# Head stacks of an attention layer: how their parts lie in DRAM, how they are loaded, and when each half is waited for

## The reference

```python
q1, q2, k, v = (split_heads(x @ W) for W in (Wq1, Wq2, Wk, Wv))   # 16 heads of 16 features
q = concatenate([q1, q2], heads)          # 32 query heads
k2, v2 = repeat(k, 2), repeat(v, 2)       # query heads 2n and 2n+1 share key head n
p = softmax(causal(q @ k2.T / 4))
y = p @ v2
y = y[:, :16] - sigmoid(x @ Wlam) * y[:, 16:]
x = layernorm(x + y @ Wo)
x = layernorm(x + shared_mlp(x) + routed_mlp(x) * comb_w)   # comb_w from a top-2 router
```

## Time and profile before

| | |
|---|---|
| median of three runs | 504.79 us |
| profiled execution, own time | 504.88 us |
| span of its instructions | 503.1 us |
| TensorE busy | 424.3 us (84%) |
| VectorE busy | 329.1 us (65%) |
| ScalarE busy | 239.1 us (48%) |
| GpSimd busy | 226.7 us (45%) |
| mean granted TensorE clock | 0.950 |
| DMA, hardware queue q1 | 34304 packets, 39.75 MB |

### The profile page before, as it was taken

One profiled execution on the slowest core, in us unless ns is written; L12 is line 12 of the kernel. 1 busy time (PEld: TensorE's weight loads), 2 busy tenths in 40 slices (PEclk: granted clock), 3 DMA queues, 4 the chain that ended last, 5 costly groups with the idle time before them and its releaser, 6 DMA issues.

```text
span 503.1 us, 10443 instructions
## 1 busy us (share of the span) xinstructions
PE 424.3 (84%) x4008; PEld 337.4 (67%) x4008; DVE 329.1 (65%) x875; ACT 239.1 (48%) x532; POOL 226.7 (45%) x283
## 2 busy tenths in 40 slices
PE   4107597799999999999899999999999988997983
PEld 4106335676688758876798668865887578766983
DVE  3504615974478577877687677857786769676674
ACT  4601284337435672548334843576255821582240
POOL 8201466427435572547434743656254721373040
PEclk9756779889999999999999999999999999999998
DMA  8892496129603680249112940377024910000000
GB/s 290 188 123 49 126 137 150 44 75 124 89 4 114 91 121 23 75 92 135 51 42 78 141 90 12 107 97 119 20 79 74 133 46 0 5 2 22 1 23 21
DMA packets 34355, 40.43 MB, mean 80 GB/s; under 512 B 3840, under 2 KB 27904, under 8 KB 34048
## 3 DMA queue, kind: packets, MB, share of 16 engines
q1 hardware_dynamic: 34304, 39.75, 43.2%
HBM read 27.94 MB, written 11.53 MB: 78 GB/s over the span
## 4 chain that ended last, share of the span: by engine, by line
PE 69%; DVE 15%; DMA 5%; ACT 5%; issue 4%; POOL 2%; SPq 1%; DVEq 0%
PE ybank L734 10%; PE ff L622 9%; PE ff L624 8%; PE ff L623 8%; DVE neg_max L990 8%; PE ring L706 5%; PE ring L685 5%; DMA k_stack<-qk_parts_dram 4%; PE ybank L622 4%; PE ybank L747 3%; PE ring L710 3%; PE ybank L623 3%; PE ybank L624 3%; ACT prob L469 2%; PE ring L680 2%
## 5 line engine op out<-in xcount | busy, mean ns | idle before, releaser
L990 DVE TENSOR_REDUCE neg_max<-ring 128x2 f32<-128x512 f32 (+3 forms) x176 | 105.7, 635 | 39.2 <-PE ring L685 37.4
L469 ACT ACTIVATE prob<-ring 128x512 f32<-128x512 f32 x192 | 100.8, 612 | 15.9 <-PE ring L706 15.8
L370 POOL TENSOR_TENSOR h_lo<-h_full,h_hi 128x256 fp32r<-128x256 f32 x72 | 53.0, 736 | 107.7 <-ACT h_hi L429 107.7
L380 POOL TENSOR_SCALAR_AFFINE_SELECT prob<-prob 128x512 f32<-128x512 f32 x128 | 83.9, 679 | 33.9 <-ACT prob L469 33.9
L622 PE MATMUL ff<-x1T_hi,wg_lo 128*128 128x256 f32 x288 | 85.8, 298 | 1.2 <-DVE h_full L1006 1.2
L624 PE MATMUL ff<-x1T_hi,wg_hi 128*128 128x256 f32 x288 | 80.5, 279 | 0.0
L623 PE MATMUL ff<-x1T_lo,wg_hi 128*128 128x256 f32 x288 | 80.5, 279 | 0.0
L680 PE MATMUL ring<-mask_b,ident_b 128*128 128x128 bf16 (+2 forms) x176 | 45.2, 257 | 32.7 <-DMA k_stack<-qk_parts_dram 26.8
L477 ACT ACTIVATE gate_t<-ff 128x256 f32<-128x256 f32 x72 | 27.6, 384 | 77.2 <-PE ff L624 74.5
L685 PE MATMUL ring<-k_stack,q_stack 96*128 96x256 bf16 (+3 forms) x512 | 60.5, 239 | 0.0
L734 PE MATMUL ybank<-prob,v_ones 128*32 128x256 f32 (+1 forms) x1024 | 56.1, 338 | 4.2 <-issue 2.8
(11 more groups left out here) (150 smaller groups left out, 947.9 us busy)
## 6 DMA issues: line engine op xcount, KB each, us to landing
q_stack<-qk_parts_dram SPq DMA_DIRECT2D x48, 256.0 KB, 9.2
qk_parts_dram<-parts SPq DMA_DIRECT2D x72, 128.0 KB
k_stack<-qk_parts_dram SPq DMA_DIRECT2D x8, 384.0 KB, 15.0
xt_raw<-xT SPq DMA_DIRECT2D x8, 256.0 KB, 2.9
k_stack<-qk_parts_dram SPq DMA_DIRECT2D x8, 256.0 KB, 11.8
xz<-x SPq DMA_DIRECT2D x8, 256.0 KB, 3.3
out<-xz SPq DMA_DIRECT2D x8, 256.0 KB, 2.2
prob<-w_gu SPq DMA_DIRECT2D x1, 1152.0 KB, 7.7
```

The source lines that it names most:

```text
L370: pool.tensor_tensor(h_lo[:, n, :], h_full[:, n % RING, :], h_hi[:, n, :].bitcast(F32), ALU.subtract).then_inc(h_lo_done, 1)
L380: pool.affine_select(out=v, in_=v, compare_op=ALU.is_ge, fill=0.0, base=0, pattern=[[0, 2], [HALF, 2], [0, 2], [1, HALF]], channel_multipl ...
L469: act.activation(prob[:, g % RING, u, :], ring[u][:, :], ACT.Exp, scale=SCALE).then_inc(exp_done, 1)
L990: dve.tensor_reduce(neg_max[:, columns.start:columns.stop, i], ring[u % RING][:, 0:len(columns) * keys].rearrange("p (h k) -> p h k", k=keys),
```

## The change

The parts of q and of k get DRAM tensors of their own, `q_parts_dram` with the two q jobs kept apart and `k_parts_dram`. In both, the eight heads of a block with 512 values each follow each other, a run of 8 KB for one feature. `q_stack` is laid out to match: first the block, then the head in it.

The slots that hold the same part are filled by one load: three copies of the high part, two of the middle one, one of the low one (`Q_RUNS`). The source of such a load repeats with a stride of zero in its outermost dimension: source `[0, 3], [8192, 16], [1, 4096]` (stride, count), destination `[8192, 48], [1, 1], [1, 4096]` for the three copies. Each covers one q job, so there are six q loads in a sequence as before, now 3 + 3 by halves, beside the three k loads, whose runs are now 8 KB.

The order of the projections becomes q (first half of the heads), k, q (second half); `Q_JOB` and `K_JOB` name them, and the host puts the weight columns in that order. The loads are in two groups with a semaphore each. `load_first_half` needs only the first two jobs, and `load_second_half` the third one. TensorE waits for the first group ahead of unit 0 and for the second ahead of unit 11. The 22 units are reordered accordingly: eleven for heads 0 to 7 (1, 2, 4 and 4 units by query tile), then the same for heads 8 to 15. The third projection moves from after unit 10 to after unit 11. At the start of the program the order on SP changes too.

```diff
-Q_PARTS = (0, 0, 0, 1, 1, 2)
-K_PARTS = (0, 1, 2, 0, 1, 0)
-SLOTS = len(Q_PARTS)
+Q_JOB, K_JOB = (0, 2), 1
+EARLY_JOBS = K_JOB + 1
+Q_RUNS = ((0, 3), (3, 2), (5, 1))
 K_RUNS = ((5, 1), (3, 2), (0, 3))
-S_JOBS = tuple((i, j) for i, heads in enumerate(S_TILE_HEADS) for j in range(HEADS // heads))
+S_JOBS = tuple((i, q * (BLOCK_HEADS // heads) + j)
+               for q in range(Q_JOBS) for i, heads in enumerate(S_TILE_HEADS) for j in range(BLOCK_HEADS // heads))
-QK_AT = (3, 6, 10)
+QK_AT = (3, 6, 11)
-        scratch = nc.dram_tensor("qk_parts_dram", [3, HEAD_DIM, BLOCK_HEADS, QK_JOBS, 2 * T], BF16, kind="Internal").ap()
+        scratch_q = nc.dram_tensor("q_parts_dram", [3, HEAD_DIM, Q_JOBS, BLOCK_HEADS, 2 * T], BF16, kind="Internal").ap()
+        scratch_k = nc.dram_tensor("k_parts_dram", [3, HEAD_DIM, BLOCK_HEADS, 2 * T], BF16, kind="Internal").ap()
...
-                for p in range(3):
-                    sp.wait_ge(parts_stored[p], (b + 1) * (16 * QK_JOBS))
-                    for s in range(SLOTS):
-                        if Q_PARTS[s] == p:
-                            sp.dma_start(q_stacks[b % STACKS][HEAD_DIM * s:HEAD_DIM * (s + 1), :, :, :], scratch[p, :, :, 0:Q_JOBS, :]).then_inc(stack_loaded, 16)
-                    s, count = K_RUNS[p]
-                    sp.dma_start(k_stacks[b % STACKS][HEAD_DIM * s:HEAD_DIM * (s + count), :, :, :],
-                                 scratch[0:count, :, :, Q_JOBS, :].rearrange("p d r t -> (p d) r t")).then_inc(stack_loaded, 16)
+            def load_q(b, q, p):
+                s, count = Q_RUNS[p]
+                sp.dma_start(q_stacks[b % STACKS][HEAD_DIM * s:HEAD_DIM * (s + count), q, :, :].rearrange("p r t -> p (r t)"),
+                             scratch_q[p, :, q, :, :].rearrange("d r t -> d (r t)").unsqueeze(0).to_broadcast([count, HEAD_DIM, BLOCK_HEADS * 2 * T])).then_inc(stack_loaded[q], 16)
+            def load_k(b, p):
+                s, count = K_RUNS[p]
+                sp.dma_start(k_stacks[b % STACKS][HEAD_DIM * s:HEAD_DIM * (s + count), :, :, :].rearrange("p r h t -> p (r h t)"),
+                             scratch_k[0:count].rearrange("p d r t -> (p d) (r t)")).then_inc(stack_loaded[0], 16)
+            def load_first_half(b):
+                if b >= STACKS:
+                    sp.wait_ge(t_full, (b - STACKS + 1) * T_UNITS)
+                for p in range(3):
+                    sp.wait_ge(parts_stored[p], (b + 1) * (16 * EARLY_JOBS))
+                    load_q(b, 0, p)
+                    load_k(b, p)
+            def load_second_half(b):
+                for p in range(3):
+                    sp.wait_ge(q_last_stored[p], (b + 1) * 16)
+                    load_q(b, 1, p)
...
-            for n, p in ((0, 0), (1, 0), (0, 1), (2, 0), (1, 1), (2, 1), (0, 2), (1, 2), (2, 2)):
+            for n, p in ((0, 0), (1, 0), (0, 1), (1, 1), (2, 0), (0, 2), (1, 2)):
                 store_part(0, n, p)
+            load_first_half(0)
+            for p in range(1, 3):
+                store_part(0, QK_JOBS - 1, p)
+            load_second_half(0)
             load_xt(1)
-            load_stacks(0)
...
+                if u % (S_UNITS // Q_JOBS) == 0:
+                    q = u // (S_UNITS // Q_JOBS)
+                    pe.wait_ge(stack_loaded[q], (b + 1) * (16 * STACK_LOADS[q]))
...
-                pe.wait_ge(stack_loaded, (i + 1) * (16 * STACK_LOADS))
...
-        "w_proj": np.concatenate([q_cols, a["attn_Wk"], a["attn_Wv"], a["attn_Wlam"]], axis=1),
+        "w_proj": np.concatenate([q_cols[:, :D], a["attn_Wk"], q_cols[:, D:], a["attn_Wv"], a["attn_Wlam"]], axis=1),
```

More of the change, by code:

```diff
@@ L41 @@
 PROJ_COLS = 4 * D + HEADS
-Q_PARTS = (0, 0, 0, 1, 1, 2)
-K_PARTS = (0, 1, 2, 0, 1, 0)
-SLOTS = len(Q_PARTS)
+Q_JOB, K_JOB = (0, 2), 1
+EARLY_JOBS = K_JOB + 1
+Q_RUNS = ((0, 3), (3, 2), (5, 1))
 K_RUNS = ((5, 1), (3, 2), (0, 3))
-STACK_LOADS = SLOTS + len(K_RUNS)
+SLOTS = sum(count for _, count in Q_RUNS)
+STACK_LOADS = (len(Q_RUNS) + len(K_RUNS), len(Q_RUNS))
 STACK_ROWS = SLOTS * HEAD_DIM
@@ L125, in build_layer @@
         rest = sb("rest", [P, REST_SLOTS, 2 * T])
-        q_stacks = [sb(f"q_stack{k}", [P, BLOCK_HEADS, Q_JOBS, 2 * T], BF16) for k in range(STACKS)]
+        q_stacks = [sb(f"q_stack{k}", [P, Q_JOBS, BLOCK_HEADS, 2 * T], BF16) for k in range(STACKS)]
         k_stacks = [sb(f"k_stack{k}", [P, BLOCK_HEADS, KEY_BLOCKS, T], BF16) for k in range(STACKS)]
@@ L189, in build_layer @@
         parts_stored = [sem(f"parts{p}_stored") for p in range(3)]
-        stack_loaded, max_loaded, out_stored = sem("stack_loaded"), sem("max_loaded"), sem("out_stored")
+        q_last_stored = [sem(f"q_last{p}_stored") for p in range(3)]
+        stack_loaded = [sem(f"stack_half{q}_loaded") for q in range(Q_JOBS)]
+        max_loaded, out_stored = sem("max_loaded"), sem("out_stored")
         consts_made, const_step = sem("consts_made"), sem("const_step")
@@ L225, in s_job, with wait_stored @@
             return i, range(j * heads, (j + 1) * heads), (i + 1) * HALF
-        def spot(column):
-            return divmod(column, Q_JOBS)
+        def wait_stored(engine, b, n, p):
+            if n < EARLY_JOBS:
+                engine.wait_ge(parts_stored[p], b * (16 * EARLY_JOBS))
+            else:
+                engine.wait_ge(q_last_stored[p], b * 16)
         def psum_order(ap):
@@ L233, in part_order @@
         def part_order(p, n):
-            view = "p (i h t) -> p h i t" if n < Q_JOBS else "p (h i t) -> p h i t"
+            view = "p (i h t) -> p h i t" if n != K_JOB else "p (h i t) -> p h i t"
             return parts[:, p, n, :].rearrange(view, h=2, i=Q_TILES)
@@ L252, in store_part @@
                 sp.wait_ge((qk_h_done, qk_m_done, qk_l_done)[p], b * QK_JOBS + n + 1)
-                sp.dma_start(scratch[p].rearrange("d r n t -> r d n t")[:, :, n, :], parts[:, p, n, :]).then_inc(parts_stored[p], 16)
+                if n == K_JOB:
+                    home = scratch_k[p].rearrange("d r t -> r d t")
+                else:
+                    home = scratch_q[p].rearrange("d j r t -> r d j t")[:, :, Q_JOB.index(n), :]
+                stored = parts_stored[p] if n < EARLY_JOBS else q_last_stored[p]
+                sp.dma_start(home, parts[:, p, n, :]).then_inc(stored, 16)
             def store_parts(b, jobs):
@@ L258, in store_parts @@
                         store_part(b, n, p)
-            def load_stacks(b):
+            def load_q(b, q, p):
[7 more added lines that the diff above has]
+            def load_first_half(b):
                 if b >= STACKS:
@@ L295, in iteration @@
                 if has_next:
-                    load_stacks(i + 1)
+                    load_first_half(i + 1)
+                    load_second_half(i + 1)
                 if is_first(i):
@@ L358, in third_part @@
                 if not is_first(b):
-                    pool.wait_ge(parts_stored[2], b * (16 * QK_JOBS))
+                    wait_stored(pool, b, n, 2)
                 pool.wait_ge(qk_m_done, b * QK_JOBS + n + 1)
@@ L442, in first_part @@
                 if not is_first(b):
-                    act.wait_ge(parts_stored[0], b * (16 * QK_JOBS))
+                    wait_stored(act, b, n, 0)
                 copy(part_order(0, n), psum_order(qk_bank(b, n)[:, :])).then_inc(qk_h_done, 1)
@@ L448, in second_part @@
                 if not is_first(b):
-                    act.wait_ge(parts_stored[1], b * (16 * QK_JOBS))
+                    wait_stored(act, b, n, 1)
                 copy(part_order(1, n), psum_order(rest_slot(b, n))).then_inc(qk_m_done, 1)
@@ L665, in q_pair @@
                 block, row = divmod(n, BLOCK_HEADS)
-                return q_stacks[b % STACKS][rows, row, block, columns]
+                return q_stacks[b % STACKS][rows, block, row, columns]
             def s_unit(b, u):
+                if u % (S_UNITS // Q_JOBS) == 0:
+                    q = u // (S_UNITS // Q_JOBS)
+                    pe.wait_ge(stack_loaded[q], (b + 1) * (16 * STACK_LOADS[q]))
                 if u == 0:
@@ L683, in s_unit @@
                 for j, c in enumerate(columns):
-                    row, block = spot(c)
-                    mm = pe.matmul(o[:, j, :], q_stacks[b % STACKS][rows, row, block, i * P:(i + 1) * P], k_stacks[b % STACKS][rows, row, block, 0:keys],
+                    block, row = divmod(c, BLOCK_HEADS)
+                    mm = pe.matmul(o[:, j, :], q_stacks[b % STACKS][rows, block, row, i * P:(i + 1) * P], k_stacks[b % STACKS][rows, row, block, 0:keys],
                                    start=False, stop=True, skip_group_check=True)
```

## The result

Four runs of the changed kernel gave 523.53 to 528.08 us, median 527.23; the kernel before gave 504.75 in the same comparison. The ratio is 1.0436 (95% interval 1.0407 to 1.0466): slower by 22 us. The forecast was 525.6, range 508 to 533. The profiled execution took 528.08 us, span 526.4, against 504.88 and 503.1, so 23.2 us are to be placed.

A forecast was written before the change was run, and what follows sets the result against it. The prediction saw only one TensorE wait to gain from, 26.8 us for a stack load at the start. To 504.88 us it added 7.5 (start), 10.3 (iteration 0 to 1), 1.5 (clock) and 1.4 (steady): 525.6, range 508 to 533.

The forecast's parts named there:

- Three and two engines per load: Stack loads with outermost source count 3 or 2 run on three or two DMA engines, each making a whole 131 kB copy.
- the sum for engine 0: Load times added up for DMA engine 0, assumed to be in every load: four 131 kB copies plus 66 kB per sequence.
- First half at 36.2, and of no use: Program start: first-half loads land at 36.2, 4.8 us ahead of 40.96, but TensorE then stands at sequence 1's projection.
- Start +7.5: Program start: sequence 1's projection begins at 50.9, not 43.86 (+7.0), plus 0.5 for slow clock; +2.3 with factor 1.
- Iteration 0 to 1, +10.3: End of iteration 0: `w_down` arrives 31.8 us after sequence 1's first stack load, not 21.3; 10.5 later less 0.24 slack.
- The pace of 25.2 GB/s for a free engine: Stack loads: an unhindered DMA engine moves 404/16 = 25.2 GB/s, so one copy takes 5.2 us.
- The factor 2 for the first load: First three-copy load of each stack: its three engines hinder each other by 2, so 10.4 us, not 5.2; chance 0.5.
- The loads that use all sixteen engines: Low-part and k loads keep sixteen engines; in the first half they add 2.3 us (57 kB) on engine 0.
- Slow clock, +1.5: After iteration 0's new stall TensorE runs at clock 0.50: Wo product +1.1 and part of the next units, +1.5 us.
- Steady iterations, +1.4: Steady iterations: loads stay hidden, the reorder costs +0.2 us in each of seven iterations, +1.4 (-2 to +3.5).
- Sum: Whole kernel: 504.88 + 7.5 + 10.3 + 1.5 + 1.4 = 525.6 us.
- The rival of all sixteen engines (499): All stack loads use sixteen engines, projection of sequence 1 starts earlier: 504.9 - 7.5 + 1.4 = 499 us; chance 0.10.

The follow-up runs named there:

- e_feature: Changed kernel with the feature (16) outermost in each load's source and the copies second, same loads and bytes, stack rows permuted: 499.25 us.
- e_rows: Changed kernel with the three-copy load filling rows 32 to 79 and the two-copy load rows 0 to 31, k loads following: 523.49 us.
- e_order: Kernel before with only the 22 units reordered by halves of heads and the third projection behind unit 11: 503.52 us, ratio 0.9984.
- e_oneload: Kernel before with only the loads of repeated slots joined (three copies, two, one), old layout, order and waits: 592.33 us, ratio 1.1721.

## Why the prediction was right, step by step

- **Three and two engines per load.** Right. It was inferred from the 0.51 of the stores; the trace has 0.19 and 0.12, and e_feature takes the cause away alone. That it is the same engines each time, with one of them in every load, no row names; the times that follow from the sum for engine 0 fit it. The quoted rule of the Trainium skill (DMA: Bandwidth & Descriptors, "Rules for kernel authors") holds here at 3 and 2.
- **First half at 36.2, and of no use.** 37.20, and TensorE stood still after four units. Right.
- **Start +7.5.** The projection came 8.9 later instead of 7.0, and the loads of sequence 1 were issued 9.5 later (69.84 for 60.33) instead of 7.5. Too small by 2.0. The low-part load was issued at 20.13 and not right after the k load at 18.51, and the landing of `xt_raw` was 11.7 us after its issue at 38.98; `xt_raw` was there at 50.67 against 49.0, which is 1.7 of it.
- **Iteration 0 to 1, +10.3.** `yT_hi` was 21.5 later, of which 9.5 were there at the issue: 12.0. Too small by 1.7. The pace of 25.2 GB/s for a free engine was nearly right (26). The factor 2 for the first load, 5.2 us in each stage, was mis-sized: other rows for that load give back 3.1 us at the start and 0.8 in this stage (e_rows). Without the factor my sum for this stage would have been 5 us, and 12 were measured. What filled the gap is a term that I priced too low. The loads that use all sixteen engines (all of k and the low part) I counted at the pace of a free engine, 2.3 us, although had such loads at 119 GB/s. From 74 to 82 all engines are busy at 154 GB/s, 1.23 MB in 8 us; at 404 GB/s this would take 3.0. So some 5 of the 7 us are there, by this estimate; no run separates it. The 10.33 us of the second `w_down` issue in SP's row are not the reason: ScalarE waits for the first `w_down` load, issued at 75.19, ahead of it.
- **Slow clock, +1.5.** The Wo product ran from 108.04 to 110.74, 2.70 for 1.45 (86.57 to 88.02): +1.2.
- **Steady iterations, +1.4.** +0.16 in each here and +0.20 in e_order, where +0.2 was forecast, but the rest of it was in two places that I had no term for: iteration 1 got shorter by 1.6 us and the last stretch longer by 1.3. In sum 0.6 in place of 1.4.
- **Sum.** 9.5 + 12.0 + 1.2 + 0.6 = 23.3 for 23.2 measured; forecast 20.7. The mechanism and both places are shown. That the time came within 2 us is in part luck: the factor 2 stood in for what the sixteen-engine loads cost, and the steady term came out 0.8 lower than forecast.
- **The rival of all sixteen engines (499).** e_feature measured 499.25, but by other terms than the rival's. The projection of sequence 1 began 7.9 us earlier (7.5 in the rival), yet the first unit of iteration 1 stood only 4.2 earlier (83.83 for 88.02); iteration 1 was another 3.2 shorter, for which the rival had no term.

The iteration 1 gain is in e_order as well, so it comes with the order of units. In the kernel before TensorE's granted clock is 0.73 from 98 to 110 us and in the changed one 0.86 in the same place (120.7 to 132.7). In e_order it is 0.88 there (97.1 to 109.1). The clock may be the link, but no run separates it.

## What to carry to other kernels

A load that repeats a source should have the repeated dimension inside, not outermost: permute the rows of the destination if need be. Here that was worth 28 us with two transfers queued behind the loads, and 11 with both ahead of them. Before joining or slowing loads, look at what stands behind them in the queue; at both places the loss came from another transfer, and moving that one ahead was worth 12 and 14 us, both together 21. An earlier start of one engine is worth nothing while its list soon needs something that was moved behind.

## What the runs showed of the hardware

- One DMA engine that is not hindered moves 26 GB/s in runs of 8 KB (78 GB/s on three, changed kernel, 30 to 36) and 25 in runs of 2 KB (e_oneload, 52 to 54). Three that fill rows 0 to 47 of a stack together moved 18 each (e_oneload, 30 to 36).
- All sixteen engines filling stacks moved 154 GB/s together from 74 to 82, 10 each, where the weights came in at 404. A share near 1 doesn't say that much is moved.
- Most issues on SP take 0.3 to 0.8 us, but one took 10.33 us in the changed kernel and one 15.83 in e_oneload, with loads on few engines pending. Both are loads over all sixteen engines, and in the program neither stands behind a wait for a semaphore. What holds SP there is not shown; the row of e_oneload:

```profile
25.69 15.83 SPq L269 DMA_DIRECT2D k_stack<-qk_parts_dram  x1
```
